# Three of the convolutions' first four products issued among the attention's last tile, with PSUM banks owned by the whole program

## The reference

```python
# part 1: attention over the batch, for every pixel
xn = groupnorm(x, 8 groups); t = conv1x1(xn, ciw) + pe
q, k, v = heads(LN(t))                       # 8 heads of 8; the 8 images are the sequence
t = softmax(q @ k.T / sqrt(8)) @ v @ wout.T + t
tn2 = LN(t); m = (tn2 @ w1.T + b1) * gelu(t @ w2.T + b2) @ w3.T + b3
x = conv1x1(m + t, cow) + x
# part 2: three steps of two 3x3 convolutions, then relu
for _ in range(3):
    h = relu(conv3x3(x, w1) + b1)
    x = x + (conv3x3(h, w2) + b2) / 3
out = relu(x)
```

## Time and profile before

| | us |
|---|---|
| median of 3 runs | 1147.93 |
| lowest and highest | 1145.34, 1148.26 |
| profiled execution, its own time | 1145.88 |
| its span in the trace | 1144.1 |
| PE, DVE, ACT, POOL busy | 1074.3, 1039.7, 651.9, 510.6 |

### The profile page before, as it was taken

One profiled execution on the slowest core, in us unless ns is written; L12 is line 12 of the kernel. 1 busy time (PEld: TensorE's weight loads), 2 busy tenths in 40 slices (PEclk: granted clock), 3 DMA queues, 4 the chain that ended last, 5 costly groups with the idle time before them and its releaser, 6 DMA issues. The chain is left out here.

```text
span 1144.1 us, 21014 instructions
## 1 busy us (share of the span) xinstructions
PE 1074.3 (94%) x7238; PEld 603.3 (53%) x7238; DVE 1039.7 (91%) x1475; ACT 651.9 (57%) x1525; POOL 510.6 (45%) x422
## 2 busy tenths in 40 slices
PE   4279999999999999999979999999999999999995
PEld 3156787777777777777643333333333333333331
DVE  5459999999999999999976999999999999999996
ACT  4567889888988898888642233253233232342332
POOL 5134555455544554455342435335344344444440
PEclk9999999999999999999998999999999999999998
DMA  8110111111111111110000000030001200030003
GB/s 303 51 37 20 38 34 34 29 38 34 33 29 39 38 29 29 38 38 11 19 20 1 1 1 1 1 75 1 1 1 25 50 1 1 1 74 1 1 1 74
DMA packets 87544, 35.83 MB, mean 31 GB/s; under 512 B 70209, under 2 KB 86850, under 8 KB 86930
## 3 DMA queue, kind: packets, MB, share of 16 engines
q1 hardware_dynamic: 85634, 33.81, 11.1%
q10 hardware_dynamic: 1040, 0.35, 0.1%
q0 software_dynamic: 768, 0.33, 0.1%
HBM read 26.09 MB, written 8.39 MB: 30 GB/s over the span
## 5 line engine op out<-in xcount | busy, mean ns | idle before, releaser
L1145 ACT ACTIVATE y<-acc,cols 128x1024 f32<-128x1024 f32 x96 | 110.2, 1207 | 267.3 <-PE acc L1137 267.3
L1127 PE MATMUL acc<-mixed_h,cwp 128*128 128x512 f32 x384 | 177.6, 605 | 0.0
L1127 PE MATMUL acc<-early,cwp 128*128 128x512 f32 x384 | 176.1, 607 | 1.5 <-PEq L423 1.5
L880 POOL TENSOR_TENSOR rstd<-var,half 128x8 f32<-128x8 f32 x32 | 80.7, 2522 | 216.4 <-DVE var L735 216.4
L1428 POOL TENSOR_TENSOR early<-xs 128x256 f32<-128x256 f32 x95 | 77.0, 810 | 160.2 <-DVE xs L1176 160.2
L1153 DVE TENSOR_TENSOR y<-y,acc 128x512 f32<-128x512 f32 x192 | 119.9, 682 | 22.0 <-ACT y L1145 21.8
L566 PE MATMUL cb<-consts,early 128*128 128x128 f32 x1024 | 133.6, 280 | 0.0
L1161 DVE TENSOR_TENSOR y<-y,acc 128x512 f32<-128x512 f32 x192 | 124.4, 684 | 8.7 <-PE acc L1137 6.7
L585 PE MATMUL cb<-consts,prod 128*128 128x128 f32 x1024 | 128.2, 273 | 2.8 <-DVE prod L534 2.1
L1127 PEld LDWEIGHTS acc<-early,cwp 128*128 128x128 f32 x384 | 70.6, 191 | 106.4 <-issue 93.8
L1127 PEld LDWEIGHTS acc<-mixed_h,cwp 128*128 128x128 f32 x384 | 69.0, 189 | 107.9 <-issue 107.9
(11 more groups left out here) (182 smaller groups left out, 1863.0 us busy)
## 6 DMA issues: line engine op xcount, KB each, us to landing
xs<-in_x SPq DMA_DIRECT2D x4, 2048.0 KB, 16.5
xa<-in_x SPq DMA_DIRECT2D x32, 256.0 KB, 2.7
xr<-in_x SPq DMA_DIRECT2D x64, 128.0 KB, 2.9
out_y<-xs SPq DMA_DIRECT2D x32, 256.0 KB, 4.7
cw<-in_L_conv_w POOLq DMA_DIRECT2D x2, 144.0 KB, 4.1
consts<-in_consts ACTq DMA_DIRECT2D x1, 192.0 KB
group<-in_consts SPq DMA_DIRECT2D x1, 64.0 KB
w1n<-in_L_conv_w ACTq DMA_DIRECT2D x1, 64.0 KB
```

The lines of the kernel that those rows point to most:

```text
L880: pool.tensor_tensor(rstd1[:, :], var1[:, :], top["half"][:, :], ALU.pow).then_inc(rstd1_done, 1)
L1127: pe.matmul(psum[PSUM_PAIR[v, q, j]][i][:, :, :], weights(v, i, j).rearrange("p n o -> p (n o)"), mixed[v][i][:, s0:s0 + WIDE, j, :], star ...
L1145: act.activation(pairs(y[i][q][:, :, :]), m1, ACT.Identity, bias=cols[:, (6, 8)[v]:(7, 9)[v]]).then_inc(m1_out[i][q], 1)
```

## The change

The eight PSUM banks are made once, in `program`, as four tensors of two banks each, and every stage takes views of them. A new function, `first_products`, issues the two matmuls of product j of (g = 0, v = 0, q = 0) into bank pair k. It is called three times in the attention's PE stream for its last tile: `first_m1` (j = 2, pair 0, the banks of `q_ps`) ahead of `pe_rstd2`, `first_m2` (j = 3, pair 1, the banks of `cb`) behind `pe_a`, and `first_m3` (j = 1, pair 2, the banks of `zb`) behind `pe_cow`. Each waits for the last reader of its banks and for the mixed chunks. In the convolution block `pe_products` returns at once for these three; the edges and the product j = 0 stay where they were.

```diff
--- before.py
+++ after.py
@@ -44,9 +44,6 @@
     with ExitStack() as ctx:
         def sb(name, shape, dt=F32):
             return ctx.enter_context(nc.sbuf_tensor(name, shape, dt))
-
-        def ps(name, shape):
-            return ctx.enter_context(nc.psum_tensor(name, shape, F32))
 
         def sem(name):
             return ctx.enter_context(nc.semaphore(name))
@@ -92,7 +89,7 @@
         gexp = sb("gexp", [P, PAIRS])
         ga = sb("ga", [P, PAIRS])
         gb = sb("gb", [P, PAIRS])
-        pt = [ps(f"pset{k}", [P, 512]) for k in range(8)]
+        pt = [top["banks"][k // 2][:, k % 2, :] for k in range(8)]
 
         core_loaded, rest_loaded, pe_done, dve_done = sem("core_loaded"), sem("rest_loaded"), sem("pe_done"), sem("dve_done")
 
@@ -464,12 +458,10 @@
         gel = sb("gel", [P, 2 * N])
         gated = sb("gated", [P, 2 * N])
 
-        q_ps = ctx.enter_context(nc.psum_tensor("q_ps", [P, 2, 2, 4 * C], F32))
-
-        cb = ctx.enter_context(nc.psum_tensor("cb", [P, 2, 512], F32))
-        zb = ctx.enter_context(nc.psum_tensor("zb", [P, 2, 512], F32))
-        b5 = ps("b5", [P, 512])
-        b7 = ps("b7", [P, 512])
+        q_ps = top["banks"][0][:, :, :].rearrange("p e (a c) -> p e a c", a=2)
+
+        cb, zb = top["banks"][1], top["banks"][2]
+        b5, b7 = top["banks"][3][:, 0, :], top["banks"][3][:, 1, :]
         b4, b2 = cb[:, 0, :], cb[:, 1, :]
         b6, b3 = zb[:, 0, :], zb[:, 1, :]
         HALF = N // 2
@@ -636,6 +628,34 @@
             for e in range(2):
                 pe.matmul((b5, b7)[e][:, :], top["w1T"][half(e), :], tn2[half(e), :], start=True, stop=True).then_inc(a_mm, 1)
 
+        def first_products(pe, j, k):
+
+            done = top["inner_done"] if j > 1 else top["outer_done"]
+            for i in range(2):
+                for c in range(2):
+                    wait(pe, done[i][c], 1)
+                pe.matmul(top["banks"][k][:, i, :], top["cw"][0][:, j, i:i + 2, :].rearrange("p n o -> p (n o)"),
+                          top["mixed_x"][i][:, 1:17, j, :], start=True, stop=False)
+
+        def first_m1(pe):
+            for g in range(2):
+                wait(pe, raw_out[g], TILES)
+            first_products(pe, 2, 0)
+
+        def first_m2(pe):
+            wait(pe, var2_done, TILES)
+            wait(pe, tn2_done, TILES)
+            wait(pe, sq2_out, TILES)
+            wait(pe, cen2_out, TILES)
+            first_products(pe, 3, 1)
+
+        def first_m3(pe):
+            wait(pe, shift_done, TILES)
+            wait(pe, z1_out, TILES)
+            for d in range(2):
+                wait(pe, gelu_out[d], TILES)
+            first_products(pe, 1, 2)
+
         def rows(ap, r):
 
             return ap.rearrange("p (e j r w) -> p r j e w", e=2, j=2, r=2)[:, r]
@@ -915,6 +935,8 @@
             if tiles[3]:
                 pe_av(pe, t - 3, 2)
             if tiles[4]:
+                if t - 4 == TILES - 1:
+                    first_m1(pe)
                 pe_rstd2(pe, t - 4)
             if tiles[3]:
                 pe_av(pe, t - 3, 3)
@@ -924,6 +946,8 @@
                 pe_z1(pe, t - 3)
             if tiles[4]:
                 pe_a(pe, t - 4)
+                if t - 4 == TILES - 1:
+                    first_m2(pe)
             if tiles[3]:
                 pe_center(pe, t - 3, (k - 3) % RING)
             if tiles[0]:
@@ -942,6 +966,8 @@
                 pe_scores_t(pe, t - 1, 2)
             if tiles[4]:
                 pe_cow(pe, t - 4, (k - 4) % RING)
+            if t - 4 == TILES - 1:
+                first_m3(pe)
 
         def act_iteration(act, t, k, tiles):
             if tiles[1]:
@@ -1075,7 +1101,7 @@
         mixed = [top["mixed_x"], [sb(f"mixed_h{i}", [P, SLOTS + 2, PRODS, DUO]) for i in range(2)]]
         h = [sb(f"h{i}", [P, SLOTS, PADW]) for i in range(2)]
         y = [[sb(f"y{i}_{q}", [P, WIDE, HW]) for q in range(NW)] for i in range(2)]
-        psum = [[ctx.enter_context(nc.psum_tensor(f"acc{k}_{i}", [P, WIDE, DUO], F32)) for i in range(2)] for k in range(4)]
+        psum = [[top["banks"][k][:, i, :].rearrange("p (s j) -> p s j", s=WIDE) for i in range(2)] for k in range(4)]
 
         def of_image(name, n):
             return [[sem(f"{name}{i}_{k}") for k in range(n)] for i in range(2)]
@@ -1118,6 +1144,8 @@
             return inner_done if j > 1 else outer_done
 
         def pe_products(pe, g, v, q, j):
+            if (g, v, q) == (0, 0, 0) and j > 0:
+                return
             if g == 0 and v == 1:
                 pe.wait_ge(zeroed, ZEROED)
             s0 = 1 + WIDE * q
@@ -1443,6 +1471,7 @@
         }
         top["mixed_x"] = [buf[:, 0:(SLOTS + 2) * PRODS * DUO].rearrange("p (s j w) -> p s j w", s=SLOTS + 2, j=PRODS)
                           for buf in top["early"]]
+        top["banks"] = [ctx.enter_context(nc.psum_tensor(f"banks{k}", [P, 2, 512], F32)) for k in range(4)]
         for name in ("inner_done", "outer_done"):
             top[name] = [[ctx.enter_context(nc.semaphore(f"{name}{i}_{c}")) for c in range(4)] for i in range(2)]
         with ExitStack() as inner:
```

## The result

| | before | changed |
|---|---|---|
| median of 3 runs, us | 1147.93 | 1138.14 |
| lowest and highest | 1145.34, 1148.26 | 1138.01, 1138.44 |
| profiled execution, its own time | 1145.88 | 1138.14 |
| its span | 1144.1 | 1136.3 |

The ratio is 0.9921, 95% interval 0.9902 to 0.9941: the changed kernel is 0.8% faster, and that is clear of the noise. The median lies inside the predicted range, 1136.5 to 1142.5. Lines of the changed kernel have other numbers: the products are L1155 (before L1127), the edges L1165 (L1137), the rrep transposes L620 (L628), the `a` matmuls L629 (L637), the gated ones L671 (L651), the last group L677 (L657); the products moved ahead are L637. All PSUM tensors are now named `banks`.

The account below looks back on a forecast made before the run. It took PE, busy for 94% of the span, as the bound. Seam start -0.5 and first stretch -6.86 make 7.4 us less: 1138.5 from the profiled execution, 1140.5 from the median, middle 1139.5; range 1136.5 to 1142.5.

Parts of the forecast that it names:

- First product free, margin 0.15: Product j=2 ahead of the rrep transposes: its 1.91 us fit PE's wait for rrep, cost 0, bounds 0 and 0.5.
- Second product costs 0.31: Product j=3 behind the `a` matmuls runs 599.01 to 600.92 and delays the gated matmuls by 0.31 us.
- The seam, start at 604.9 between the bounds 604.45 and 604.98: Between attention and convolution: PE's next start, 605.43 before, comes at 604.9, as no engine continues until the last finishes.
- The clock does not fall: PE's clock stays full around the seam, giving 1.65 us on the attention's last matmul groups.
- B: Rival: the clock falls at 598.7 all the same, returns at 608.9; 2.6 us less, up to 5 more; chance 0.08.
- First stretch 5.56: Convolution's first stretch keeps one product and 32 edge records: 5.56 us instead of 12.42, 6.86 less.
- Nothing late behind it: Second half's products: ACT's m1 keeps its margin and POOL's last chunk comes about 607.6, needed at 610.5.
- C: Rival: in the convolutions DVE, 91% busy, sets the pace and PE's lead becomes waits, 1145.9; chance 0.04.
- D: Rival: the clock falls as in B and does not return at 608.9; 3.6 us slower, 1149.4; chance 0.03.
- The sum, 7.4 us: PE reaches the second half's products at 610.5 instead of 617.85: 0.5 from the seam plus 6.86 from the stretch.
- The median: Whole time: 1138.5 from the profiled execution, 1140.5 from the median of before; the middle, 1139.5, was taken.

Follow-up runs that it names:

- m1_only: Changed kernel with only product j=2 kept ahead of the rrep transposes, the other two given back to the convolution block; median 1142.02 us.
- m1_m2: Changed kernel with products j=2 and j=3 kept ahead and j=1 given back to the convolution block; median 1140.73 us.
- again: Changed kernel with the convolution block issuing all four products again, so the three moved ones are computed twice; median 1144.65 us.
- changed_again: The changed kernel itself, unaltered, run five more times; median 1138.60 us, ratio to before 0.9921 to 0.9946.
- filled: Changed kernel plus 30 matmuls whose results nobody reads, in PE's waits in the setup and first tiles; median 1134.82 us.
- m2_only: Changed kernel with only product j=3 kept ahead, behind the `a` matmuls, the other two given back to the convolution block; median 1144.62 us.
- m3_only: Changed kernel with only product j=1 kept ahead, behind the attention's last group, the other two given back to the convolution block; median 1145.88 us.
- m2_m3: Changed kernel with products j=3 and j=1 kept ahead and j=2 given back to the convolution block; median 1143.77 us.
- m1_late: Changed kernel with product j=2 moved behind the rrep transposes instead of ahead of them; median 1141.58 us.

## Why the prediction was right

Step by step, the prediction's number first:

- **First product free, margin 0.15.** L677 started at 593.75, the product at 594.34, and it took 1.98, to 596.32; L620 started at 596.47, against ACT's rrep as before. Right. What the prediction did not say is that this one product carries the clock: `m1_only` measures 3.35 us for it on top of its 1.72.
- **Second product costs 0.31.** It ran from 598.97, and L671 started at 600.88 (600.92 predicted; the whole trace is 0.04 earlier). DVE's gated ended at 599.11 + 1.41 = 600.52. Right. Its net worth is 6.50 - 5.07 = 1.43, against 1.72 - 0.31 = 1.41.
- **The seam, start at 604.9 between the bounds 604.45 and 604.98.** 604.92, and `m1_m2` shows why: it counts from PE's own product. The choice for this bound was right, and so was its reason.
- **The clock does not fall.** 1.00 in all windows; 1.65 us ahead of the seam and 1.7 behind it came back, and `again` confirms the sum of clock and costs with 2.19 against 2.2. This was a judgement in the prediction (0.85 against 0.08 for B), not worked out, and the traces with the wait open show on what it hung: with the first product elsewhere the clock falls as in B. It was cheaper than B had it: B took its 10.2 us from the one trace of before, and the low level then lasted 3.4 or 6.8 us.
- **First stretch 5.56.** 610.40 - 604.92 = 5.48; in the chain's view 610.47 - 604.92 = 5.55.
- **Nothing late behind it.** PE's table of waits has one entry behind the seam:

```profile
PE banks L1155 <- PEq L420: 0.5, 1, 0.5
```

  ACT's m1 ended at 607.97 + 2.31 = 610.28, 0.12 ahead of PE's need, the same as before (617.66 to 617.78). C falls, D too.
- **The sum, 7.4 us.** 7.38 at the second half's products.
- **The median.** From the profiled execution the prediction was 1138.5, from the median 1140.5, and it took 1139.5. Measured: 1138.14, 9.8 us below the median of before and 7.7 below its profiled execution. So the number from the profiled execution was right to 0.4 us, and the one from the median was 2.4 too high. The weak term is that middle, which no row supports. The later traces show one term of 1.2 to 2.4 us that can lie between two executions of one kernel, the clock at the start of the program, and one of the next five runs of the changed kernel was 1.7 us above the others. Whether the two slower runs of before had it, or a longer loss at the seam, they cannot tell, as these runs have no trace. But the 58 later executions of the kernel before, run beside the experiments, have a mean granted clock on record: ten had 0.993, as the profiled one, and took 1145.3 on average; twenty had 0.989 and took 1147.6. Seven of the eight of the changed kernel had 0.997 or 0.996. So the profiled execution of before had lost less of the clock than most, and the median gains more (9.8 us here, 8.3 in `changed_again`) than the 7.4 that its trace explains. That such terms differ between few runs was not in the prediction; its range covered it, and that part is luck.

## What to carry to other kernels

Work moved into an engine's wait is worth its own length less what it sticks out: 1.72, 1.43 and 0.84 us here for three products of 1.72, the last because a seam counts from the last engine to finish. On TensorE a filled wait can be worth more than the work in it, since a clock that falls in it or soon behind it makes what follows dear; the same matmuls put behind the wait instead of into it had neither the cover nor, in the trace, the clock. And where whole times spread by more than the effect, a stretch between two fixed instructions in one trace resolves a tenth of a us as long as the clock stays up in it (16.65, 16.65 and 16.66 in the changed kernel, `changed_again` and `filled`).

## What the runs showed of the hardware that I had not expected

- After a fall the low level lasted 10.2 us before, and 6.8, 6.8, 6.8 and 3.4 us in `m2_only`, `m3_only`, `m2_m3` and `m1_late`, where PE waited less behind the fall. That this is the reason is not shown: at the program's start it lasted 6.8 us in three traces and 10.2 or 10.3 in three others of the same instructions. The moment of the fall moved as well, from 1.6 to 4.9 us behind the start of the same group. What a fall costs is not known from one trace.
- In the first 65 us the granted clock reads 1.00 in the traces of before and changed, while the qkv groups take 2.08 us there (the last at 63.74 before) and 1.13 later (from 74.22). The column shows neither a low level there nor the rise between the two, so at a program's start the durations tell the clock, not that column. In `filled` the same groups take 1.13 from 50.66 us on.
- 30 unread matmuls took 3.8 us off the median. Matmuls for nobody are worth a try wherever TensorE's short groups lie on a chain that fills a pipeline.
